# Cross-attention with exact float32 scores: score products packed into two whole-array passes and a row-tiled third

## What is computed

```python
q, k, v = norm(x) @ Wq, context @ Wk, context @ Wv          # per head, 64 wide
attn = softmax(einsum('bhsd,bhld->bhsl', q, k) * 64 ** -0.5)
x = x + einsum('bhsl,bhld->bhsd', attn, v) @ Wo + bo
flat = norm(x)
p = softmax(flat @ router_w + router_b)                      # 8 experts, the two best weigh
x = x + gelu(flat @ sw1 + sb1) @ sw2 + sb2 + sum_e w_e * (gelu(flat @ rw1[e] + rb1[e]) @ rw2[e] + rb2[e])
```

## Time and profile before

| | us |
|---|---|
| runs: median, lowest, highest of 3 | 492.44, 491.92, 496.47 |
| the profiled execution: its span | 489.6 |
| PE, DVE, POOL, ACT busy in it | 464.8, 371.8, 283.0, 153.2 |

### The profile page before, as it was taken

The page is one execution under the profiler, slowest core; times in us unless marked ns, Lnnn a source line. Parts: engine busy times, 40 slices in busy tenths (PEclk is TensorE's granted clock), DMA queues, the critical chain, the costliest instruction groups (busy, mean ns, idle before and its releaser), DMA issues.

```text
span 489.6 us, 7181 instructions
## 1 busy us (share of the span) xinstructions
PE 464.8 (95%) x2545; PEld 330.6 (68%) x2545; DVE 371.8 (76%) x665; ACT 153.2 (31%) x190; POOL 283.0 (58%) x170
## 2 busy tenths in 40 slices
PE   8889999999999999999999599999999999977996
PEld 7766666777776666667767367676766666765784
DVE  4977778796859776967678976968587568979775
ACT  3442323232313332322223032323132444353241
POOL 5737675756355757563466347554557750764873
PEclk9999999999999999999999799999999999998899
DMA  8200001000000000000000030000000000000000
GB/s 291 77 1 1 1 0 52 1 1 2 0 1 1 0 1 0 2 1 0 1 0 1 1 98 0 1 1 1 0 2 1 0 1 0 1 1 1 5 18 22
DMA packets 5250, 7.27 MB, mean 15 GB/s; under 512 B 892, under 2 KB 3872, under 8 KB 5216
## 3 DMA queue, kind: packets, MB, share of 16 engines
q1 hardware_dynamic: 4672, 6.29, 4.1%
q10 hardware_dynamic: 544, 0.52, 0.3%
...
...
## 4 chain that ended last, share of the span: by engine, by line
PE 84%; DVE 11%; issue 2%; POOL 1%; ACT 1%; DVEq 0%; POOLq 0%
PE ps L1001 19%; PE ps L922 10%; PE ps L984 10%; PE ps L985 9%; PE ps L986 9%; PE ps L837 6%; PE ps L839 6%; PE ps L838 6%; PE ps L934 2%; PE ps L928 2%; PE ps L940 1%; DVE maxes L697 1%; PE ps L895 1%; DVE ties L757 1%; PE ps L844 1%
## 5 line engine op out<-in xcount | busy, mean ns | idle before, releaser
L579 ACT ACTIVATE probs<-ps 128x1024 f32<-128x1024 f32 (+1 forms) x112 | 107.8, 963 | 267.2 <-PE ps L986 259.6
L423 POOL TENSOR_TENSOR work<-work,probs 128x1024 f32<-128x1024 f32 x60 | 143.1, 2385 | 61.0 <-ACT probs L579 59.8
L697 DVE TENSOR_REDUCE maxes<-ps 128x1 f32<-128x402 f32 x256 | 136.6, 568 | 23.3 <-PE ps L922 22.5
L1001 PE MATMUL ps<-probs,v_sb 128*64 128x256 f32 (+1 forms) x832 | 103.7, 387 | 0.0
L984 PE MATMUL ps<-g_hi,ctxT_hi 97*128 97x512 f32 (+1 forms) x208 | 87.1, 419 | 0.4 <-issue 0.4
L922 PE MATMUL ps<-ctxT_hi,g_hi 96*128 96x402 f32 x256 | 80.6, 367 | 4.2 <-DVE g_lo L622 2.8
L1001 PEld LDWEIGHTS ps<-probs,v_sb 128*64 128x64 f32 (+1 forms) x832 | 54.1, 136 | 43.7 <-issue 21.2
L985 PE MATMUL ps<-g_lo,ctxT_hi 96*128 96x512 f32 (+1 forms) x208 | 82.5, 397 | 0.0
L986 PE MATMUL ps<-g_hi,ctxT_lo 96*128 96x512 f32 (+1 forms) x208 | 82.2, 395 | 0.0
L421 POOL TENSOR_TENSOR work<-probs 128x1024 f32<-128x1024 f32 x15 | 35.8, 2386 | 77.4 <-issue 73.0
L534 POOL TENSOR_TENSOR g_lo<-probs,g_hi 128x512 fp32r<-128x512 f32 x34 | 45.6, 1362 | 36.5 <-DVE g_hi L805 35.3
...
## 6 DMA issues: line engine op xcount, KB each, us to landing
...
out_dram<-x_sb SPq DMA_DIRECT2D x2, 256.0 KB, 2.1
...
early<-in_L_xattn_Wq_dram SPq DMA_DIRECT2D x1, 256.0 KB, 3.1
wo_sb<-in_L_xattn_Wo_dram SPq DMA_DIRECT2D x1, 256.0 KB, 6.9
...
```

The costliest lines, as they stand in the source:

```text
L423: ops.tensor_tensor(acc, acc, pr, ALU.add).then_inc(summed, 1)
L579: nc.scalar.activation(probs[0:rows, n % 4, 0:wide, :], s, ACT.Exp, scale=SCALE).then_inc(probs_ready, 1)
L697: v.tensor_reduce(maxes[:, p % 2, i * T + t, blk:blk + 1], src[:, 0:BW], AX.X, ALU.max).then_inc(ring_taken, 1)
L1001: ins = mm(o_bank[DH * i:DH * (i + 1), :], v_sb[0:rows, c, h * DH:(h + 1) * DH], probs[0:rows, n % 4, j, i * S:(i + 1) * S], start=(c == 0 ...
```

## The change

- The three products of 96 rows (288 rows and the row of ones) are packed: `ctxA` holds the high part's 96 rows and 32 of the rest, `ctxB` the high part again and the next 32, so that two passes of 128 rows (`full`) do 256 of the 288 rows, and `ctxC` the last 32 with the row of ones. The third pass (`row`) has 33 rows in a tile of 64; even chunks lie in partitions 0 to 32, odd ones in 64 to 96. g is packed alike (`gA`, `gB`, `gC`), its spare rows come out of the g product itself. `v` and `v0` take the same packed context in three whole-array passes (`project`).
- The context comes transposed from the host, and so do Wq and Wk; no transposes of them are left on PE. ACT makes the high part (`high`), POOL the rest (`rest`), and SP's queue moves rows between partitions by DMAs from SBUF to SBUF: six per batch (`pack_ctx`), three per pair of heads (`pack_g`), four for Wv. One raw buffer instead of two.
- Units are taken in groups of two (up to four chunks), across pairs: all `full` passes, all `row` passes, then the values of the group before. Ring tasks are put ahead of `full` passes alone. 56 groups.
- v0 is interleaved with the maxima of the first pair from the fourth on, and waits for the packing.
- The negated maximum is computed and copied twice (for both row tiles). The reciprocal is taken in PSUM. `rank` and `best` of the router come in different groups. The high part of `split` moves from DVE to ACT. g and the experts' splits share one buffer of 4 pairs, 6 splits instead of 8.

```diff
-COST = {"max": 1.3, "v": 1.2, "turn": 2.4, "g": 2.4, "shift": 1.2, "y": 1.0, "yt": 6.0, "xt": 1.5, "sums": 4.5,
+COST = {"max": 1.3, "v": 1.2, "g": 2.4, "shift": 1.8, "y": 1.0, "yt": 6.0, "xt": 1.5, "sums": 4.0,
...
-            nb, np_ = order[n + 1]
-            if np_ == 0:
-                for g in range(per_batch):
-                    put[5 + 2 * g] = turns[nb * per_batch + g]
-            put[len(maxima) - 3] = ("g", nb, np_)
+            put[len(maxima) - 3] = ("g",) + order[n + 1]
         for m, task in enumerate(maxima):
             tasks.append(task)
-            if n == 0 and m % 2 and n_v0 < chunks:
+            if n == 0 and m >= 3 and n_v0 < chunks:
...
+    sequence = [(b, p, u) for b, p in order for u in range(n_units)]
+    groups = [sequence[i:i + 2] for i in range(0, len(sequence), 2)]
...
+        done = ((n + 1) * n_units - 1) // 2 + 1
+        after[done].append(("ring", ("sums", b, p)))
+        if p == pairs - 1:
+            after[done + 1].append(("ring", ("y", b)))
+            after[done + 2].append(("ring", ("yt", b)))
+            after[done + 4].append(("norm", b))
+            after[done + 6].append(("ring", ("xt", b)))
+            if (b + 1) % (batches // halves) == 0:
+                h = (b + 1) * halves // batches - 1
+                after[done + 7] += [("ring", ("router", h)), ("exp", h)]
+                after[done + 8].append(("rank", h))
+                after[done + 9].append(("best", h))
...
+    for n, group in enumerate(groups):
+        for kind, w in parts("full", group):
+            b, p, u, j = w
+            if p == 0 and b:
+                main.append(("ring", ("v", b, units[u][j])))
+            main.append((kind, w))
+        main += parts("row", group)
+        if n:
+            main += values(held)
+            held = []
+            for w in groups[n - 1]:
+                if w[2] == 0 and w != groups[n - 1][0]:
+                    held.append(w)
+                else:
+                    main += values([w])
+        main += after[n]
+    main += values(held + groups[-1])
...
-        if kind == "scores" or kind == "values" and last != "values":
-            need = last_of[("shift", w[0], w[1])] if kind == "scores" else 0
+            need = last_of[("shift", w[0], w[1])]
...
+        ctxA = sb("ctxA", [P, 2, L], F32R)
+        ctxB = sb("ctxB", [P, 2, L], F32R)
+        ctxC = sb("ctxC", [P, 2, CP], F32R)
...
-        g_hi_all = sb("g_hi", [P, 2, HEADS, S], F32R)
-        g_lo_all = sb("g_lo", [P, 2, HEADS, S], F32R)
-        g_hi, g_lo = g_hi_all[0:C + 1], g_lo_all[0:C]
+        g_all = sb("g_all", [P, 3 * GS, 2 * S], F32R)
+        gA, gB, gC = g_all[:, 0:GS], g_all[:, GS:2 * GS], g_all[:, 2 * GS:3 * GS]
...
+            def pack_wv():
+                sp.wait_ge(wv_hi_ready, 1)
+                for dst, r0, src in ((wvA, C, 0), (wvB, C, CR), (wvC[:, 0], 0, CA), (wvC[:, 1], 2 * CR, CA)):
+                    sp.dma_start(dst[r0:r0 + CR, :].bitcast(F32), wvA[src:src + CR, :].bitcast(F32)
+                                 ).then_inc(s_wpack, 16)
+            def pack_ctx(b):
+                k = b % 2
+                sp.wait_ge(ctx_hi_ready, 2 * (b + 1))
+                sp.dma_start(ctxB[0:C, k, :].bitcast(F32), ctxA[0:C, k, :].bitcast(F32)).then_inc(s_pack[b], 16)
+                sp.wait_ge(ctx_rest_ready, 2 * (b + 1))
+                rest = raw[:, 1, :]
+                sp.dma_start(ctxA[C:P, k, :].bitcast(F32), rest[0:CR, :]).then_inc(s_pack[b], 16)
+                sp.dma_start(ctxB[C:P, k, :].bitcast(F32), rest[CR:2 * CR, :]).then_inc(s_pack[b], 16)
+                pairs = rest[CA:C, 0:FULL * P].rearrange("p (k two c) -> p k two c", two=2, c=P)
+                for i in range(2):
+                    sp.dma_start(ctxC[2 * CR * i:2 * CR * i + CR, k, 0:FULL // 2 * P].bitcast(F32).rearrange(
+                        "p (k c) -> p k c", c=P), pairs[:, :, i, :]).then_inc(s_pack[b], 16)
+                sp.dma_start(ctxC[0:CR, k, FULL // 2 * P:FULL // 2 * P + REST].bitcast(F32),
+                             rest[CA:C, FULL * P:L]).then_inc(s_pack[b], 16)
+            def load_ctx(b):
+                sp.dma_start(ctx_raw, ctxT[b]).then_inc(s_ctx[b], 16)
+            def pack_g(pair):
+                k, b, p = pair % GS, *divmod(pair, PAIRS)
+                sp.wait_ge(ring_taken, ring_no[("g", b, p)] + 1)
+                for dst, r0, src in ((gB, C, CR), (gC, 0, CA), (gC, 2 * CR, CA)):
+                    sp.dma_start(dst[r0:r0 + CR, k, :].bitcast(F32), gA[src:src + CR, k, :].bitcast(F32)
+                                 ).then_inc(s_gpack[k], 16)
+            sp.dma_start(early[:], WqkT).then_inc(s_wqk, 16)
+            sp.dma_start(wv_sb, Wv).then_inc(s_wv, 16)
+            sp.dma_start(rw_sb[:], router_w).then_inc(s_rw, 16)
+            pack_wv()
+            pack_ctx(0)
+            load_ctx(1)
+            sp.dma_start(w1_sb[:, 0:E], rw1.rearrange("e d h -> d e h")).then_inc(s_w1, 16)
+            sp.dma_start(w1_sb[:, E], sw1).then_inc(s_w1, 16)
+            pack_g(0)
...
+            g.tensor_copy(wvA[0:C], wv_sb).then_inc(wv_hi_ready, 1)
+            pool.wait_ge(wv_hi_ready, 1)
+            g.tensor_tensor(wvB[0:C], wv_sb, wvA[0:C].bitcast(F32), ALU.subtract).then_inc(w_split, 1)
+            then_own(g.memset(ctxC[:].bitcast(F32), 0.0))
+            for r in (CR, 3 * CR):
+                g.memset(ctxC[r:r + 1, :, :].bitcast(F32), 1.0).then_inc(consts_ready, 1)
+            pool.wait_ge(consts_ready, 3)
+            rest(0)
...
+            def high(b, parts):
+                act.wait_ge(s_ctx[b], 16 * parts)
+                if b >= 2:
+                    act.wait_ge(scores_ready, unit_no(b - 1, 0, 0))
+                for i in range(2):
+                    cs = slice(i * HH, min((i + 1) * HH, L))
+                    nc.scalar.copy(ctxA[0:C, b % 2, cs], ctx_raw[:, cs]).then_inc(ctx_hi_ready, 1)
...
+                elif kind == "split":
+                    n, e = w, items[w][1]
+                    if n == 0:
+                        act.wait_ge(scores_ready, LAST_UNIT)
+                    if n >= SPLITS:
+                        act.wait_ge(w2_done, n - SPLITS + 1)
+                    if e == E:
+                        act.wait_ge(hid_ready, n + 1)
+                    else:
+                        act.wait_ge(hidw_ready, weighed[n])
+                    nc.scalar.copy(hid_hi[:, n % SPLITS, :], activations(n)).then_inc(hid_hi_ready, 1)
...
+                            for col in (CR, C):
+                                v.tensor_reduce(neg_max[:, p % 2, :, col], maxes[:, p % 2, :, :], AX.X, ALU.max,
+                                                negate=True).then_inc(max_ready, 1)
                     elif w[0] == "shift":
                         p = w[2]
-                        v.tensor_copy(g_hi[C:C + 1, b % 2, 2 * p:2 * p + 2, :],
-                                      src[C:C + 1, :].rearrange("p (h s) -> p h s", h=2)).then_inc(ring_taken, 1)
+                        pair = b * PAIRS + p
+                        v.tensor_copy(gC[CR:CR + 1, pair % GS, :], src[CR:CR + 1, :])
+                        v.tensor_copy(gC[C:C + 1, pair % GS, :], src[C:C + 1, :]).then_inc(ring_taken, 1)
...
+                        rden = src[:, 0:S]
+                        v.reciprocal(rden, rden).then_inc(rden_ready, 1)
+                        dve.wait_ge(rden_ready, pair + 1)
                         dve.wait_ge(o_raw_ready, pair + 1)
-                        v.tensor_tensor(oT[:, b % 2, w[2], :], o_raw[:], rden[:], ALU.mult).then_inc(o_taken, 1)
+                        v.tensor_tensor(oT[:, b % 2, w[2], :], o_raw[:], rden, ALU.mult).then_inc(ring_taken, 1)
...
+            def project(dst, b, c):
+                rows = P if c < FULL else REST
+                ks, cs = slice(c * P, c * P + rows), slice(c // 2 * P, c // 2 * P + rows)
+                mm(dst[0:rows, :], ctxA[:, b % 2, ks], wvA[:], start=True, stop=False)
+                mm(dst[0:rows, :], ctxB[:, b % 2, ks], wvB[:], start=False, stop=False)
+                return mm(dst[0:rows, :], ctxC[:, b % 2, cs], wvC[:, c % 2], start=False, stop=True)
...
+                        pe.wait_ge(s_pack[b], 96)
+                        ins = project(dst, b, w[2])
...
-                    mm(dst, ctxT_hi[:, b % 2, ks], gh, start=True, stop=False)
-                    mm(dst, ctxT_hi[0:C, b % 2, ks], gl, start=False, stop=False)
-                    ins = mm(dst, ctxT_lo[:, b % 2, ks], gh[0:C], start=False, stop=True)
+                    mm(dst, ctxA[:, b % 2, ks], gA[:, k, :], start=True, stop=False)
+                    mm(dst, ctxB[:, b % 2, ks], gB[:, k, :], start=False, stop=False)
+                elif kind == "row":
+                    b, p, u, j = w
+                    n, c, k = unit_no(b, p, u), UNITS[u][j], (b * PAIRS + p) % GS
+                    if j == 0:
+                        pe.wait_ge(ring_taken, ring_no[("shift", b, p)] + 1)
```

(8 more changed lines are left out.)

325 lines of the change are left out of this document (127 added, 198 removed).

## The result

The changed kernel takes 526.67 us (median; 525.48 to 527.34) against 492.18 of the kernel before on the same chip. The ratio is 1.065, with an interval of 1.059 to 1.072: slower, outside the forecast's range, and on the other side. The profiled execution of the changed kernel has a span of 524.6 us, 35.0 over the 489.6 of before.

A forecast was written before the change was run, and what follows sets the result against it. PE was taken as the bound in the main stage, with DVE close behind. 489.6 - 22.6 + 9 - 10.4 + 1.5 + 7 + 9 - 3 - 2 = 478.1, plus 2.8: 481 us, range 466 to 499.

The forecast's parts named there:

- steps 1 and 2: Score passes on PE: overlapping row tiles save 22.6 us; further changes of the array's mode cost a net 9.
- the forecast's 2.3 for eight value blocks fewer: Value products on PE: groups fall from 64 to 56, at 0.29 us each, saving 2.3 us.
- the Trainium skill's 77% of full overlap: Score passes: two row tiles at that share gain 1.53x, saving 15.8 us in place of 22.6, end 488 us.
- step 3: Context transposes leave PE (-6.2 us) and their splits leave DVE (-4.2), together -10.4 us.
- ACT's copies (+1.5): Two 801-column high-part copies per batch, queued on ACT ahead of exponentials, cost 0 to 5 us, taken as +1.5.
- step 4: Main stage: DVE's work stays level but it starves in dark stretches; stalls in 50 groups cost 0 to 16, taken +7 us.
- step 5: Start: PE waits for the packing before v0, with a lower clock behind it; +9 us (4 to 12).
- step 6: Router's ranking split over two groups saves 3 us; experts' casts moved from DVE to ACT save 2.
- A: Score passes: row tiles don't overlap at one column per cycle, so 504 us, slower; chance 0.13.
- B: Main stage: DVE becomes the bound and PE's savings become waits for the ring, 493 us, no change; chance 0.22.
- C: All small costs (mode switches, bunching, start) come at their low ends: 464 us; chance 0.15.
- the last two pairs gain in any case: Last two pairs: maxima run 1.8 pairs ahead, so hardly any are left there and these pairs gain even if DVE binds.

The follow-up runs named there:

- Experiment 8: Kernel before, with the context transposes of batches 2 and 3 nearly all cut: 486.5 us, ratio 0.987.
- experiment 15: Changed kernel, with DVE's maxima reading 2 of 402 columns: 513.09 us, ratio 1.037 to the kernel before.
- experiment 6: Changed kernel, with the reciprocal written to SBUF again and its ring bank free after it: 528.34 us, ratio 1.073 to the kernel before.
- experiment 9: Changed kernel, with the sums of a pair put ahead of the value products: 515.43 us, ratio 1.048 to the kernel before.
- experiment 2: Changed kernel, with POOL's additions cut to two columns: 512.11 us, ratio 1.037 to the kernel before.
- experiment 5: Changed kernel, with ring tasks also placed between row passes and value products: 538.98 us, ratio 1.094 to the kernel before.
- experiment 10: Changed kernel, with sums ahead of the value products and g and shift held back to a group's last chunk: 517.10 us, ratio 1.050.
- experiment 12: Changed kernel, with the experts' high-part casts back on DVE: 526.81 us, ratio 1.069 to the kernel before.
- experiment 17: Changed kernel, with v0 behind all maxima, sums ahead of values and the last batch's ranking one turn earlier: 505.33 us, ratio 1.024.
- experiment 4: Changed kernel, with all third passes in the upper row tile: 546.7 us, ratio 1.107 to the kernel before.

## Why the prediction was wrong

**Score passes and mode changes (steps 1 and 2): right.** The forecast was 22.6 - 9 = 13.6 us net. Measured on one calm group: 0.28 us for a group of four chunks, of which there are 40, and by the same rows (one slot of 0.235 saved, 0.19 spent on the further change) 0.05 for each of the 16 groups of three: about 12, and 14 with the forecast's 2.3 for eight value blocks fewer. The estimate by the Trainium skill's 77% of full overlap ("TensorE: Matmul & The Clock Gate", Measured speedup vs the span model) isn't borne out for two tiles of 33 rows: (0.66 - 0.19) / 4 = 0.12 us each is full overlap, and in the trace the two passes of a chunk pair start 3 ns apart.

**Transposes (step 3): right as far as shown.** Experiment 8 prices two batches of the three: the forecast's share is 5 to 6 us, the time fell by about 6 (3 to 10), and the trace shows 2.8 us of PE's work and 1.9 of its waits gone. The forecast's sum held 2.9 and 2.8 for these. ACT's copies (+1.5) weren't priced by a run.

**DVE (step 4): the failed step, in mechanism and size.** The step said that DVE would starve in the dark stretch and be late with the maxima, 0 to 0.3 us in 50 groups, +7. DVE does starve. But experiment 15 shows that its total work isn't the main matter, and the waits of the trace stand behind a few long tasks: the multiplication, the shift copies, g. Between the ring tasks of two chunks PE used to have three passes, 0.705 us, and now has two, 0.47 us; so it reaches the fourth task sooner, while the bank under reciprocal and multiplication is held for 2.2 us, longer than the 1.8 of before. That it is this shorter distance that makes the waits is read from the trace; no run put the third pass's time back between the tasks. The multiplication's own gain, 1.37 to 0.42 us and forecast rightly, was of no use there. Experiments 6 and 9 fit this: freeing the bank alone moved the wait, placing the work beside the values removed it (-8.4 by the ratios), and experiment 2 leaves the waits as they are without POOL's additions. The middle stage was to shrink by some 18 us (steps 1 to 4 and the router, less the first pair) and grew by 9.4. Of these 28 us, 15.1 are idle time of PE, and about 4 the clock behind it (6.5 us against 2.5). The rest is some 9 us of busy time more than the steps leave. Most of it is waiting too, too short to be booked as idle: at the full clock the next pass starts 0.248 us behind a maximum's on average, idle time left out, where it was 0.215 before, about 7 us over the 209 maxima of this stage, since a record of 0.35 us covers a later start of the next. With DVE's maxima cut (experiment 15) it is 0.222, so about 5 of these us follow DVE's load; and there PE's busy time at full clock is 15.5 us below that of the kernel before with the same cut, of the 19 that steps 1 to 3 promised on PE for this stage.

**The first pair: no step at all.** It was taken to gain like the others and cost 11 us. The xn wait of 5.45 us and the clock behind it (0.50 + 0.23 of two windows, 2.9 us) are the larger part. I weighed ACT's copies of the next context (+1.5) and never asked who on DVE waits for POOL's difference. In experiments 5, 9, 10 and 15 a pair of normalizations of the later pairs came to lie beside POOL's work, and PE got a new wait of 3 to 6 us; in the changed kernel itself they took 0.34 to 0.92 us each there. The Trainium skill states the rule in "SBUF — State Buffer", "SBUF: two separate sides": the pair of ports that DVE and GpSimd share goes to whichever starts first, for its whole instruction, and the other waits. The trace agrees, and goes further (last section).

**Start (step 5): right.** The term was +9 (4 to 12), and the first score pass comes 10.6 us later than before. Idle until 23.5 (forecast 21): POOL 1.3 us later than summed, and the last packing transfers took 5.1 us and not 3.8. The first scores at 39.1 (35.5): 2.5 of the 3.6 us are this later start; the chain from the last maximum over the negated maxima to the shift, 2.3 us from 36.8 on, I left out; the passes between took 1.2 less than summed. The lower clock behind the wait was there (0.67).

**Router and experts (step 6): wrong sign.** Around the router the pair still takes 33.0 us (32.0 before); the ranking in two pieces met POOL's additions in twos, and its last operations took 1.80 and 2.37 us. In the experts' stage the casts brought no gain (experiment 12), and the ranking one turn later costs 5 to 6 us (experiment 17), which the step didn't price.

**The rivals.** A is refuted (experiment 4). B was nearest, in that PE's savings became waits for the ring, but it asked for DVE as the bound, which experiment 15 excludes (with 97 us less on DVE the later pairs fall by 2.6), and it capped the loss at the gain: with 493 it could not see a kernel that is slower by 35. C's low ends came nowhere. What no rival held is that new waits bring the lower clock with them; the forecast priced that only at the start. The check "the last two pairs gain in any case" held where PE alone counts: from the first pass of pair 14 to the last value product are 32.7 us for 34.1, of which PE then gives back 1.2 in the wait for the last sums.
